# A recurrence whose products move 16 columns instead of 32

## What is computed

```
def cell(h, x):
    gi = x @ W_ih + b_ih
    gh = h @ W_hh + b_hh
    i_r, i_z, i_n = jnp.split(gi, 3, axis=-1)
    h_r, h_z, h_n = jnp.split(gh, 3, axis=-1)
    r = jax.nn.sigmoid(i_r + h_r)
    z = jax.nn.sigmoid(i_z + h_z)
    n = jnp.tanh(i_n + r * h_n)
    h_new = (1.0 - z) * n + z * h
    return (h_new, h_new)
...
h = jax.nn.silu(jnp.einsum('td,ehd->teh', xf, w1) + b1)
y = jnp.einsum('teh,edh->ted', h, w2) + b2
out = jnp.einsum('ted,te->td', y, comb)
```

## Time and profile before

| | |
|---|---|
| median of 3 runs | 2149.39 us (2143.58 to 2150.28) |
| the profiled execution: its own time | 2148.9 us |
| its span | 2146.8 us |
| start of the first product of the recurrence | 948.0 us |
| mean granted clock of PE over the span | 0.947 |
| PE busy over the span | 1933.3 us (90%) |
| DVE, ACT busy | 1346.2 us (63%), 936.4 us (44%) |

### The profile page before, as it was taken

The page is one execution under the profiler, slowest core; times in us unless marked ns, Lnnn a source line. Parts: engine busy times, 40 slices in busy tenths (PEclk is TensorE's granted clock), DMA queues, the critical chain, the costliest instruction groups (busy, mean ns, idle before and its releaser), DMA issues.

```text
span 2146.8 us, 82157 instructions
## 1 busy us (share of the span) xinstructions
PE 1933.3 (90%) x34302; PEld 1687.2 (79%) x34302; DVE 1346.2 (63%) x5134; ACT 936.4 (44%) x3370; POOL 115.5 (5%) x189
## 2 busy tenths in 40 slices
PE   5889989989998695976689999999999999999999
PEld 3677677677675574866579989989899899898998
DVE  4566665665666107955567776676767766767664
ACT  1355445545545221223335444455454444554443
POOL 0021021021011220000000000000000000000000
PEclk9999999999999897986679999999999999999999
DMA  6000000000000471220000000000000000000000
GB/s 259 1 1 0 0 0 0 0 0 0 0 0 2 152 254 57 74 72 12 9 18 18 18 13 18 18 28 4 28 18 18 13 18 18 28 4 28 4 13 11
DMA packets 54435, 66.14 MB, mean 31 GB/s; under 512 B 4928, under 2 KB 46272, under 8 KB 53104
## 3 DMA queue, kind: packets, MB, share of 16 engines
q1 hardware_dynamic: 50608, 46.96, 6.5%
q0 software_dynamic: 3520, 14.69, 2.2%
HBM read 44.83 MB, written 16.81 MB: 29 GB/s over the span
## 4 chain that ended last, share of the span: by engine, by line
PE 46%; DVE 7%; issue 2%; ACT 1%; DMA 0%; DVEq 0%; ACTq 0%
PE ps L1339 26%; PE ps L1294 10%; PE ps L1273 10%; DVE dh L1470 1%; ACT nn L1390 1%; DVE hn L1463 1%; DVE dh L1476 1%; DVE nxt L1479 1%; DVE nxt L1482 1%; DVE tn L1447 1%; DVE rn L1459 1%; PE ps L1326 0%; DVE h L1480 0%; DVE ns L1472 0%; DVE tb L1556 0%
## 5 line engine op out<-in xcount | busy, mean ns | idle before, releaser
L1339 PE MATMUL ps<-nxt,whf 128*128 128x32 f16 x24576 | 660.5, 177 | 79.3 <-DVE nxt L1482 73.2
L1339 PEld LDWEIGHTS ps<-nxt,whf 128*128 128x128 f16 x24576 | 650.7, 96 | 99.4 <-DVE nxt L1482 88.2
L1390 ACT ACTIVATE rz<-s,sc 128x32 f32<-128x32 f32 x512 | 164.7, 322 | 469.0 <-DVE s L1447 467.8
L1273 PE MATMUL ps<-cur,w1f 128*128 128x256 f16 x2112 | 274.0, 275 | 0.0
L1294 PE MATMUL ps<-hh,w2f 128*128 128x256 f16 x2112 | 265.8, 273 | 0.0
L1294 PEld LDWEIGHTS ps<-hh,w2f 128*128 128x128 f16 x2112 | 205.6, 98 | 23.7
L1447 DVE TENSOR_REDUCE s<-ps 128x32 f32<-128x64 f32 x512 | 114.9, 224 | 165.5 <-PE ps L1339 163.3
L1273 PEld LDWEIGHTS ps<-cur,w1f 128*128 128x128 f16 x2112 | 199.5, 98 | 23.1
L965 PE MATMUL ps<-x1T,wi 128*128 x768 | 175.6, 392 | 21.4 <-DMA wi<-in_W_ih 14.1
L965 PEld LDWEIGHTS ps<-x1T,wi 128*128 128x128 f32 x768 | 150.5, 197 | 46.2 <-issue 24.0
L471 PE MATMUL ps<-kz,rot 128*128 128x256 f32 x512 | 158.0, 391 | 0.0
(11 more groups left out here) (205 smaller groups left out, 2811.2 us busy)
## 6 DMA issues: line engine op xcount, KB each, us to landing
gi_d<-stage SPq DMA_DIRECT2D x96, 128.0 KB, 1.7
gi<-gi_d SPq DMA_DIRECT2D x16, 768.0 KB, 4.9
w1f<-in_w1T POOLq DMA_DIRECT2D x4, 1408.0 KB, 8.7
xall<-in_x SPq DMA_DIRECT2D x4, 1024.0 KB, 9.1
x1T<-in_xT SPq DMA_DIRECT2D x1, 4096.0 KB, 21.9
w2f<-in_w2T POOLq DMA_DIRECT2D x8, 512.0 KB, 4.6
out<-x1T SPq DMA_DIRECT2D x8, 512.0 KB, 3.2
wi<-in_W_ih SPq DMA_DIRECT2D x1, 3072.0 KB, 11.9
```

Of the source, the lines that this page charges most:

```text
L1273: last = nc.tensor.matmul(ps[:, 6 + n % 2, 0:TT], w[:, wp, i % NHC * P:(i % NHC + 1) * P], cur[:, k, hq, :, :].rearrange("p s b -> p (s b) ...
L1339: last = nc.tensor.matmul(ps[:, bank, g * WIDE * 2 * B:(g + 1) * WIDE * 2 * B], whp[:, k, w, q, g * P:(g + 1) * P], h, start=False, stop=( ...
L1390: nc.scalar.activation(o.rearrange("p g b -> p (g b)"), i_.rearrange("p g b -> p (g b)"), func, scale=scale).then_inc(done, 1)
```

## The change

One constant goes from 2 to 1:

```
-WIDE = 2
+WIDE = 1
```

## The result

The changed kernel is slower: 2166.18 us median of 4 runs (2164.78 to 2168.41), against 2148.73 us (2143.58 to 2150.28) for the kernel before, measured beside it; the ratio is 1.0088, with a 95% interval of 1.007 to 1.0107. The forecast was 2168.0, range 2151 to 2190. The profiled execution has a span of 2162.7 us, against 2146.8; it was the fastest of the four (2164.78 us).

A forecast was written before the change was run, and what follows sets the result against it. The loop through PE, DVE and ACT bounds the light steps, PE the full ones. Terms 1.4 + 5 + 13.5 - 0.5 = +19.4 us on the profiled 2148.9 gave 2168 us, range 2151 to 2190.

The forecast's parts named there:

- The products are not faster: The 24,576 products: halving the columns to 16 leaves their distance from start to start at 25 ns.
- The clock is what it costs: Fewer columns moved lower the granted clock in the first tile and in later tiles' steps of few 256-column matmuls; sum +19.4 us.
- first tile, all low: First tile: all its steps at the low clock, 4.33 us against a mean of 4.29; +1.4 us (0 to +1.4).
- second tile: Second tile: clock falls in three steps, half the low-clock cost of the 23-matmul step, four small ones; +5 us (0 to +7).
- third to eighth tile: Steps 7 to 11 of these six tiles: 2.6 us of clock falls each, less two paid now; +13.5 us (+4 to +28).
- last product: Last product's way to PSUM, 169 for 176 ns, counted in 77 steps where the loop sets the length; 0.5 us off.
- Those of being right: First tile at clock 0.50; nearly every later tile with steps 7 to 11 below 1 and steps of 5.0 us or more.
- sign of being wrong: First tile's mean clock above 0.6, product bursts under 2.5 us, or a clock under 1 among the steps of 18.
- low clock in the full steps: Rival: clock stays low also in steps of 18 and 19 wide matmuls, +2.1 us each; mostly 2185 to 2260 us; chance 0.07.
- I take the columns, at 4 to 1: Across PE's steps, the granted clock goes by columns moved per microsecond, not PE's busy time; odds 4 to 1.
- No effect: Rival: the clock goes by busy time or pauses alone, so falls stay as they were; 2148.5 us, chance 0.12.
- Closer products: Rival: products of 16 columns follow in under 25 ns, about 20 us gained for each nanosecond; chance 0.04.

## Why the prediction was right

**The products are not faster** was right to the digit: 25.1 ns from start to start before and after, and the router's 16 columns had shown it. The last product's way to PSUM went from 176 to 169 ns, as the earlier trace rows had it. At the low clock the gain was larger than the 7 ns: the first tile's steps are 4.321 us, for 4.334 at the low clock before. PSUM's layout at zero: right, by the kernel with narrow light steps in the old layout.

**The clock is what it costs** was right, and the two kernels with one part of the change each place the loss. In the light steps it is all there (1.0086 of 1.0088), in the full ones it is not to be told from zero.

**The terms of the sum**, against the tiles:

| term | forecast | measured |
|---|---|---|
| first tile, all low | +1.4 | +1.0 |
| second tile | +5 | +5.2 |
| third to eighth tile | +13.5 | +9.3 |
| last product | -0.5 | within these |
| sum | +19.4 | +15.5 (medians of runs: +17.5) |

The first tile is at 0.50 as forecast; the difference is the 13 ns a step just named. The second tile's size can be relied on: the changed kernel and the two experiments that leave its light steps narrow and unfilled take 146.08, 146.09 and 146.10 us. In it the parts came differently from the working and met at the same sum: the steps of 12 to 14 took 4.76 to 5.31 us, and the 23-matmul step 6.47 us, +1.5 where 1.4 was put.

The third term came out too large in this trace. I charged each tile a third of what a low clock costs its 23-matmul step, 0.9 us; there it was at most 0.14 over its 4.92, since the clock was back before that step had got far. The 13-matmul steps are what the tiles lost: step 8 was hit in all six, by 0.43 to 1.00 us, step 10 in five, though in two of these it had been hit before too, and took 0.4 and 0.5 us less than then. Two falls came where I had put none, a step 2 of 6.04 us for 4.38 in the fourth tile and a step 1 of 5.29 for 4.30 in the fifth. A pause of 0.42 us stands ahead of the first one's products, and one of 0.37 us inside the second one's.

But this is one execution, the fastest of four, and other traces size the term otherwise. The kernel with 40 narrow fillers is the changed kernel from the second tile on, and its third to eighth tile take 13.0 us more than before; the kernel with narrow light steps alone, 10.5. There the clock does stay low into the 23-matmul step, in three of six tiles and in two. The fourth tile of the kernel with 40 fillers, steps 10 and 11:

```profile
1421.32 2.70 PE L1349 MATMUL ps<-nxt,whf 128*128 128x16 f16 x96 [0.81 <-DVE nxt L1492]
...
1424.04 2.77 PE L1277 MATMUL ps<-cur,w1f 128*128 128x256 f16 x12
1426.60 2.75 PE L1349 MATMUL ps<-nxt,whf 128*128 128x16 f16 x96
...
1429.37 1.49 PE L1277 MATMUL ps<-cur,w1f 128*128 128x256 f16 x6
...
1433.05 1.10 PE L1349 MATMUL ps<-nxt,whf 128*128 128x16 f16 x38
```

Step 11 took 1433.05 - 1426.60 = 6.45 us for 4.92. So the third of a 23-matmul step was not a wrong term; how often that step is hit differs from one execution to the next, and one trace can't size it to a few us. That the total came within 2 us of the median owes something to luck.

**Slips in the working** that leave the forecast where it was: the terms of 2.6 us add to 2.54; the lower bound takes 1 us for the second tile, whose own bound is 0; 0.109 + 0.11 is 0.219. The longest pause between two bursts of the trace before is 1.70 us, not 1.6.

**The signs.** Those of being right came, but for the seventh tile, whose 13-matmul steps took 4.59 and 4.82 us and not 5.0. One sign of being wrong came too: a clock under 1 among the steps of 18. It is the fall in step 2 of the fourth tile shown above, and there are two in the kernel with narrow full steps. None made the next step longer by more than 0.05 us, and the full steps behind had none, so the rival of a low clock in the full steps has a small part in the loss, 1.7 us in this trace.

**The reason was half right.** "I take the columns, at 4 to 1" holds against busy time and pauses, each of which is excluded as the only cause from both sides: PE never idle at a clock of 0.50, and PE idle four parts in ten at 1.00. But columns a microsecond, averaged over a step, was the wrong measure, though it ordered the kinds of steps rightly here. It failed once it was asked for a number: 830 a microsecond stayed low where 710 had risen. What measure of the columns would order all these kernels no run here settles, and it stays open.

**The rivals.** No effect (0.12): out, by the ratio. The low clock in the full steps: one fall at their edge, none in steps 12 to 31. Closer products: out. By the formula in the Trainium skill ("TensorE: Matmul & The Clock Gate", "Back-to-back issue gap") 16 and 32 columns would have differed by 6.6 ns, and they don't. The table under that formula, which the prediction left out, gives a floor of about 25 ns from start to start for 1 to 64 columns; the traces agree at 16, 32 and 48 columns, and not at 64, with 29.7 ns. The same page's rule on long idle gaps ("Why this matters for your kernels") names a cause that doesn't occur here: the clock fell with no pause over 1.7 us, it stayed low over 125 us without any pause, and it stayed high with three copies and a pause of 1.6 us in each step.

## What to carry to other kernels

Work that nobody reads may be paying for the clock: before narrowing a matmul that is bound by its distance from start to start, read the granted clock of the stretches where PE waits or moves little, and price a fall by the widest matmuls that stand behind it, not by those that are narrowed. Here columns up to 48 were free at the full clock, and using that room (three copies, or idle wide matmuls in the pauses) was worth more than saving them: they gained 0.16% and 0.28%, where saving them lost 0.88%. A busy PE is not a PE at its full clock: here, what it moved told more.

## What the runs showed of the hardware

- TensorE's clock stayed at its low level (1.2 GHz, 0.50) over 125 us in which PE had no pause at all, with bursts of 96 matmuls of 16 columns and 8 matmuls of 256 columns by turns; with 14 of them it was at 2.4 GHz, and so it was with PE busy 77.18 us of 125 in bursts of 48-column matmuls alone.
- Columns of zeros, half of each product's 32, keep the clock as well as data do: 0.64 and 0.64 over the same 125 us.
- A matmul with weights of its own, 128x128 float16, follows the last in 25.1 ns with 16, 32 or 48 columns at the full clock, and in 29.7 ns with 64. At the low clock it was 26.8 ns with 32 and (2.73 - 0.18)/95 = 26.8 ns with 16 too, while the 48 columns of the first step took (3.94 - 0.2)/95 = 39 ns.
